# Cross attention: the projected queries of a slot are copied whole to SBUF before they are split

## The reference

```python
# x (8, 1024, 512), ctx (8, 64, 512), 16 heads of 32
Q = (x @ w_q.T).reshape(B, S, 16, 32).transpose(0, 2, 1, 3)
K = (ctx @ w_k.T).reshape(B, -1, 16, 32).transpose(0, 2, 1, 3)
V = (ctx @ w_v.T).reshape(B, -1, 16, 32).transpose(0, 2, 1, 3)
scores = jnp.einsum('bhqd,bhkd->bhqk', Q, K) / np.sqrt(32)
attn = jax.nn.softmax(scores, axis=-1)
c = jnp.einsum('bhqk,bhkd->bhqd', attn, V).transpose(0, 2, 1, 3).reshape(B, S, 512)
y = c @ w_o.T + b_o + x
mu, var = mean(y), mean((y - mu) ** 2)        # over the last axis
out = (y - mu) * rsqrt(var + 1e-5) * gamma + beta
```

## Time and profile before

| | us |
|---|---|
| median of 3 runs | 547.06 (547.06 to 550.45) |
| the profiled execution | 547.24 |
| its span | 545.3 |
| PE busy | 530.1 |
| DVE / POOL / ACT busy | 434.7 / 421.7 / 381.7 |

### The profile page before, as it was taken

One profiled execution on the slowest core, in us unless ns is written; L12 is line 12 of the kernel. 1 busy time (PEld: TensorE's weight loads), 2 busy tenths in 40 slices (PEclk: granted clock), 3 DMA queues, 4 the chain that ended last, 5 costly groups with the idle time before them and its releaser, 6 DMA issues.

```text
span 545.3 us, 12514 instructions
## 1 busy us (share of the span) xinstructions
PE 530.1 (97%) x4522; PEld 401.3 (74%) x4522; DVE 434.7 (80%) x877; ACT 381.7 (70%) x739; POOL 421.7 (77%) x387
## 2 busy tenths in 40 slices
PE   8999999999999999999999999999999999999994
PEld 6765587778777777777787778777877877787663
DVE  7876768778877877787778778877877787778897
ACT  7647767767676777677677767676777677666683
POOL 1726868888888888888888888888888888877755
PEclk9999999999999999999999999999999999999998
DMA  8943224333333332333244323333333332222112
GB/s 310 273 146 92 82 83 129 91 105 120 109 90 126 120 101 93 127 125 102 85 128 129 103 84 124 114 109 99 121 108 95 120 121 64 66 78 82 46 68 110
DMA packets 56750, 61.11 MB, mean 112 GB/s; under 512 B 29169, under 2 KB 29169, under 8 KB 56689
## 3 DMA queue, kind: packets, MB, share of 16 engines
q1 hardware_dynamic: 56688, 60.32, 35.3%
HBM read 39.58 MB, written 16.78 MB: 103 GB/s over the span
## 4 chain that ended last, share of the span: by engine, by line
PE 93%; DVE 2%; issue 2%; ACT 1%; DMA 1%; SPq 0%; DVEq 0%; ACTq 0%
PE ps_q L420 32%; PE ps_o L426 28%; PE ps_s L379 12%; PE ps_s L352 8%; PE ps_q L286 5%; PE ps_s L363 3%; PE ps_o L286 3%; PE ps_s L286 2%; PE ps_s L293 1%; DMA max_rows<-max_turned 1%; DVE stats L775 1%; DVE z L771 1%; DVE y L797 0%; DVE q_lo L686 0%; ACT q_hi L509 0%
## 5 line engine op out<-in xcount | busy, mean ns | idle before, releaser
L420 PE MATMUL ps_q<-x_hi,wq_lo 64*128 64x512 f32 x448 | 179.3, 400 | 4.8 <-DVE q_lo L686 0.4
L426 PE MATMUL ps_o<-wo_hi,c_lo 64*128 64x512 f32 x448 | 181.0, 404 | 0.0
L426 PE MATMUL ps_o<-wo_hi,c_hi 64*128 64x512 f32 x448 | 175.3, 391 | 0.0
L420 PE MATMUL ps_q<-x_lo,wq_hi 64*128 64x512 f32 x448 | 175.2, 391 | 0.0
L420 PE MATMUL ps_q<-x_hi,wq_hi 64*128 64x512 f32 x448 | 175.1, 391 | 0.0
L426 PE MATMUL ps_o<-wo_lo,c_hi 64*128 64x512 f32 x448 | 174.7, 390 | 0.0
L420 PEld LDWEIGHTS ps_q<-x_hi,wq_lo 64*128 64x128 f32 x448 | 82.7, 185 | 57.1 <-DVE z L771 51.7
L928 POOL TENSOR_TENSOR y<-y,gamma_row 128x512 f32<-128x512 f32 x60 | 78.3, 1306 | 58.7 <-ACT y L574 58.7
L906 POOL TENSOR_TENSOR c_lo<-c_raw,c_hi 128x512 fp32r<-128x512 f32 x63 | 81.3, 1291 | 27.5 <-ACT c_hi L509 27.5
L771 DVE TENSOR_TENSOR z<-ps_o,x_raw 128x512 f32<-128x512 f32 x59 | 40.8, 692 | 73.7 <-PE ps_o L426 73.3
L900 POOL TENSOR_TENSOR x_lo<-xT_raw,x_hi 128x512 fp32r<-128x512 f32 x60 | 77.8, 1297 | 12.5 <-ACT x_hi L509 12.5
(11 more groups left out here) (106 smaller groups left out, 1088.8 us busy)
## 6 DMA issues: line engine op xcount, KB each, us to landing
xT_raw<-in_xT SPq DMA_DIRECT2D x64, 256.0 KB, 2.9
x_raw<-in_x SPq DMA_DIRECT2D x64, 256.0 KB, 2.8
out<-y SPq DMA_DIRECT2D x64, 256.0 KB, 2.0
max_rows<-max_turned SPq DMA_DIRECT2D x128, 16.0 KB
ctx_raw<-in_ctxT SPq DMA_DIRECT2D x4, 256.0 KB, 4.6
wk_raw<-in_wkT SPq DMA_DIRECT2D x4, 256.0 KB, 4.8
wq_raw<-in_wqT SPq DMA_DIRECT2D x4, 256.0 KB, 5.8
wv_raw<-in_wvT SPq DMA_DIRECT2D x4, 256.0 KB, 6.8
```

Of the source, the lines that this page charges most:

```text
L420: return nc.tensor.matmul(ps_q[:, 0, :], w[l][half, k, dims], x_[r][half, qc % 2, k, :], start=(half is lower and k == 0 and step == 0), s ...
L426: return nc.tensor.matmul(ps_o[:, 0, :], cx[l][half, k, tile], wo[r][half, k, :], start=(half is upper and k == 0 and step == 0), stop=(ha ...
```

## The change

From slot 8 on (`COPIED`), ACT first copies the projected queries whole from the bank `ps_q` to `q_raw` in SBUF (`copy_queries`, one more ACT instruction per slot, 56 in all). PE waits for that copy (`q_copied`) instead of for `q_lo` before it begins the next projection. `q_hi` and `q_lo` are both made from `q_raw`. The lists of all engines are also rearranged. On ACT `normalise` moves behind the inversion of the sums, the exponentials ahead of `negate_max`, and the copy stands ahead of the inverse deviation. On DVE `q_lo` moves from the end of a slot to behind the transpose of the scores, and `divide` directly behind it; the statistics move behind `turn_max`. On POOL `c_lo` moves ahead of `add_bias`. At the end `store(62)` stands ahead of `store(63)`.

```diff
--- before.py
+++ after.py
@@ -24,6 +24,7 @@
     OUT_LAG = 7
     SPLIT_AHEAD = 5
     BY_VECTOR = (57, 58, 61, 63)
+    COPIED = OUT_LAG + 1
     WARM = 10
     SCALE = float(DK) ** -0.5
     EPS = 1e-5
@@ -73,6 +74,7 @@
         xT_raw = sb("xT_raw", [P, KT, CHUNK], fp32)
         x_hi, x_lo = sb("x_hi", [P, 2, KT, CHUNK], fp32r), sb("x_lo", [P, 2, KT, CHUNK], fp32r)
         q_hi, q_lo = sb("q_hi", [P, 2, CHUNK], fp32r), sb("q_lo", [P, 2, CHUNK], fp32r)
+        q_raw = sb("q_raw", [P, CHUNK], fp32)
 
         turned = sb("turned", [P, 2 * CHUNK], fp32)
 
@@ -146,7 +148,8 @@
         ctx_lo_done, wk_lo_done, wq_lo_done, wv_lo_done, wo_lo_done = (
             sem(f"{n}_lo_done") for n in ("ctx", "wk", "wq", "wv", "wo"))
         x_hi_done, x_lo_done = sem("x_hi_done"), sem("x_lo_done")
-        q_product, q_hi_done, q_lo_done = sem("q_product"), sem("q_hi_done"), sem("q_lo_done")
+        q_product, q_copied, q_hi_done, q_lo_done = (
+            sem(n) for n in ("q_product", "q_copied", "q_hi_done", "q_lo_done"))
         scores_done, turned_done, half_max_done = sem("scores_done"), sem("turned_done"), sem("half_max_done")
         upper_max_done, row_max_done, max_hi_done = sem("upper_max_done"), sem("row_max_done"), sem("max_hi_done")
         max_lo_done, max_turned_done = sem("max_lo_done"), sem("max_turned_done")
@@ -272,7 +275,7 @@
                 next_keys(t)
             fill_max_rows(SLOTS - 1)
 
-            for i in (55, 56, 57, 58, 59, 60, 61, 63, 62):
+            for i in (55, 56, 57, 58, 59, 60, 61, 62, 63):
                 store(i)
             for s in range(4):
                 sp.wait_ge(y_stored[s], 16 * TILES // 4)
@@ -303,9 +306,16 @@
                     if k == KT - 1:
                         mm.then_inc(keys_product, 1)
 
+            def queries_left(n):
+
+                if n >= COPIED:
+                    pe.wait_ge(q_copied, n - COPIED + 1)
+                else:
+                    wait(pe, q_lo_done, n + 1)
+
             def project_queries(n):
                 c, g = divmod(n, G)
-                wait(pe, q_lo_done, n)
+                queries_left(n - 1)
                 if g == 0 and c > 0:
                     pe.wait_ge(x_lo_done, KT * (c + 1))
                 for k in range(KT):
@@ -387,7 +397,7 @@
 
                 if ks[0] == 0:
                     if i == TILES - OUT_LAG:
-                        pe.wait_ge(q_lo_done, SLOTS)
+                        queries_left(SLOTS - 1)
                     elif i >= TILES - 2:
                         pe.wait_ge(c_raw_done, 62)
                     elif i < TILES - OUT_LAG:
@@ -527,8 +537,17 @@
 
             def queries_to_hi(n):
                 wait(act, scores_done, n - 1)
+                if n >= COPIED:
+                    act.wait_ge(q_copied, n - COPIED + 1)
+                    to_hi(q_hi[:, n % 2, :], q_raw[:, :]).then_inc(q_hi_done, 1)
+                else:
+                    act.wait_ge(q_product, n + 1)
+                    to_hi(q_hi[:, n % 2, :], ps_q[:, 0, :]).then_inc(q_hi_done, 1)
+
+            def copy_queries(n):
                 act.wait_ge(q_product, n + 1)
-                to_hi(q_hi[:, n % 2, :], ps_q[:, 0, :]).then_inc(q_hi_done, 1)
+                act.wait_ge(q_lo_done, n)
+                nc.scalar.activation(q_raw[:, :], ps_q[:, 0, :], ACT.Copy).then_inc(q_copied, 1)
 
             def negate_max(n):
                 act.wait_ge(row_max_done, n + 1)
@@ -632,23 +651,24 @@
 
             for t in range(OUT_LAG, SLOTS - 1):
                 i = t - OUT_LAG - 1
+                log_sums(t - 3)
+                invert_sums(t - 3)
                 if i >= 1:
                     normalise(i - 1)
-                log_sums(t - 3)
-                invert_sums(t - 3)
                 if t + SPLIT_AHEAD < SLOTS:
                     split_x(t + SPLIT_AHEAD)
+                exponentiate(t - 2)
                 negate_max(t - 1)
-                exponentiate(t - 2)
                 context_to_hi(t - 3)
+                copy_queries(t + 1)
                 if i >= 0:
                     invert_deviation(i)
                 queries_to_hi(t + 1)
 
 
-            normalise(54)
             log_sums(60)
             invert_sums(60)
+            normalise(54)
             exponentiate(61)
             context_to_hi(60)
             invert_deviation(55)
@@ -697,7 +717,8 @@
 
             def queries_to_lo(n):
                 dve.wait_ge(q_hi_done, n + 1)
-                to_lo(q_lo[:, n % 2, :], ps_q[:, 0, :], q_hi[:, n % 2, :]).then_inc(q_lo_done, 1)
+                to_lo(q_lo[:, n % 2, :], q_raw[:, :] if n >= COPIED else ps_q[:, 0, :], q_hi[:, n % 2, :]
+                      ).then_inc(q_lo_done, 1)
 
             for t in (kbd_hi, kbd_lo):
                 for half in range(2):
@@ -819,25 +840,27 @@
                 i = t - OUT_LAG
                 if i >= 1:
                     turn_scores(t - 1)
-                    half_maxima(t - 1)
+                    queries_to_lo(t)
                 divide(t - 3)
                 if i >= 1:
+                    half_maxima(t - 1)
                     fold_halves(t - 1)
+                turn_max(t - 1)
+                if i >= 1:
                     statistics(i - 1)
-                turn_max(t - 1)
                 add_residual(i)
-                queries_to_lo(t + 1)
 
 
             turn_scores(61)
+            queries_to_lo(62)
+            divide(59)
             half_maxima(61)
-            divide(59)
             fold_halves(61)
             turn_max(61)
             statistics(54)
             add_residual(55)
+            statistics(55)
             queries_to_lo(63)
-            statistics(55)
             turn_scores(62)
             divide(60)
             half_maxima(62)
@@ -950,8 +973,8 @@
                     scale(i - 1)
                 if t + SPLIT_AHEAD < SLOTS:
                     split_x(t + SPLIT_AHEAD)
+                context_to_lo(t - 3)
                 add_bias(t - 1)
-                context_to_lo(t - 3)
                 if i >= 0:
                     shift_mean(i)
```

## The result

| | before | after |
|---|---|---|
| median (6 runs each) | 547.06 | 556.96 |
| profiled execution | 547.24 | 558.03 |
| its span | 545.3 | 556.1 |
| PE / POOL busy | 530.1 / 421.7 | 535.9 / 442.4 |

The ratio after to before is 1.0174, with a 95% interval of 1.0144 to 1.0204: slower by 1.7%, where 551 us and 0.8% were forecast.

What follows compares the result with a forecast made beforehand. PE, waiting for `q_lo`, was taken to bound the kernel; afterwards POOL's loop would: 50 × 8.00 − 1.6 − 393.5 = +4.9, less 0.8 for 5 other slots, on 547.24: 551 us, range 539 to 560 (8 in 10).

Steps and rivals of the forecast that it cites:

- What bound the kernel before, and what was removed: PE waits for `q_lo` behind each combination; the copy removes 0.15 us in 55 slots, −8.3 us, slot 7.72.
- The copy on ACT, cost 0: One more 0.60 us ACT instruction per slot fits into ACT's 0.75 us wait; the logarithm stays near 1.20.
- DVE, cost 0: `divide` ends near 3.8 instead of 4.05, so PE's scores don't wait; up to 0.1 per slot if late.
- the hold: DVE's `q_lo`, now with two SBUF operands, and POOL's instructions wait for each other's end: 0.40 us per slot on POOL.
- The price that decides: `q_lo` reading both operands from SBUF always meets a running POOL instruction, lengthening POOL's loop by 0.40 to about 8.00 us.
- POOL's loop without a hold: Closed loop from `shift_mean` through ACT's `normalise` and back: 7.59 us, 0.13 under PE's 7.72, so not binding.
- 1.2 or more as a sign: If the forecast is right, `q_lo` on DVE shows a mean near 1.2 us or more instead of 0.69.
- PE's slack, 1.6 us once: POOL's lateness reaches PE only through ACT, DVE and z, whose idle time absorbs 1.6 us, once.
- The step that failed: In the tail, later scaling and the swapped last stores each cost under 1 us, taken as 0.
- No hold at all (539): Rival: POOL is not delayed, all 55 slots run at 7.72, 539 us; chance 0.16.
- The full hold (565): Rival: `q_lo` keeps POOL out for all 0.69 us, loop 8.28, +18, 565 us; chance 0.15 for 556 and more.

Runs made afterwards that it cites:

- experiment 1: Changed kernel, but DVE's `q_lo` (slots 8 to 62) compares with one operand from PSUM, leaving out the true `q_lo`: 541.53 us, ratio 0.9889 to the kernel before.
- experiment 2: Changed kernel, but POOL adds the bias to only 32 of 512 columns: 539.79 us, ratio 0.9863 to the kernel before.
- experiment 4: Changed kernel, computing everything, with `scale`, ACT's `normalise` and SP's stores moved later, and POOL's tail reordered: 539.85 us, ratio 0.9856 to the kernel before.
- runs 5 and 6: Kernel before plus one unused DVE instruction per slot ahead of z: a subtraction with two SBUF operands (555.95 us), then a transpose with one (547.3 us).
- Experiment 3: Kernel before with one move alone, ACT's `normalise` behind the inversion of the sums, in loop and tail: 551.16 us, ratio 1.0079.
- experiment 7: Changed kernel with SP's stores behind the copies of the maxima and `c_lo(60)` and tile 55's shift ahead of `scale(55)`: 554.2 us, ratio 1.0125 to the kernel before.

## Why the prediction was right or wrong

**What bound the kernel before, and what was removed: right.** PE's 0.15 us per slot behind `q_lo` was real and went away wherever nothing else came in its place: 1.02 us behind the combination and slots of 7.72 in experiments 1, 2 and 4, and in the changed kernel's own first slots.

**The copy on ACT, cost 0: right.** It takes 0.60 us and ends 0.26 into the slot; the logarithm still starts at 1.20 in experiment 1. In the changed kernel it starts at 1.65, because ACT waits for the late statistics.

**DVE, cost 0: right in experiments 1 and 4, not quite in the changed kernel.** With z late by 0.8 us by the hold's loop, DVE's list is late too, and the division again holds PE's scores. It doesn't add to the slot, because POOL sets its length anyway; it only shows as another place where PE waits out the same time.

**The price that decides: the mechanism right, the size too small.** POOL's loop without a hold was put at 7.59, and the slots of 7.72 in experiment 1, in which POOL is idle for 1.06 us around `normalise` instead of the 0.93 of the closed loop, agree: 7.72 less the spare 0.13 is 7.59. The hold was put at 0.40 and is 0.45: I let the shorter `q_lo` (0.69 against 0.75) end 0.49 behind POOL's instruction, and it ends 0.54 behind it, as the longer ones did. 8.04 against 8.00 is 2 us over 50 slots. `q_lo` takes 1.02 us, where I had named 1.2 or more as a sign. The page "SBUF — State Buffer" of the Trainium skill, section "Who interferes with whom", names the right pair of instructions, and runs 5 and 6 bear it out. By the words "fully blocks" of that page of the Trainium skill it would be 0.69 (an estimate, with the length of `q_lo`); the changed kernel's trace shows 0.45 to 0.48 added to POOL's addition of the bias (1.29 alone), and no slot of any run more than 0.52.

**PE's slack, 1.6 us once: right.** `normalise` drifted from 2.97 to 4.65 into the slot over the first six slots, by 0.31 to 0.36 in each, before PE felt it. That is 1.68 us. (The part of z in it was 0.64 by the rows, 0.38 against 1.02, and not 0.5; the sum came out all the same.)

**The step that failed: "In the tail, scaling comes later and the last stores are swapped; both are smaller than 1 us, and I take 0."** The tail costs 2.6 us (less 0.6 behind it, which goes with the order of the last stores: 19.9 to 20.0 us pass from the last combination to the end in the five runs that have the new order, 20.5 to 20.6 in the five that have the old one). I had not followed `normalise`'s 2.8 us through POOL's list to `c_lo(60)`, from there by the single `c_raw` to `divide(61)`, and down DVE's list to the statistics of tile 56. Experiment 3 shows this by the one move, experiment 7 that it can be mended. Nor had I walked SP's queue: the store of y waits for `scale` and stands ahead of the copies of the maxima, which are issued 0.94 us later by it. That leaves no room for the odd copy that takes 4.5 us, and one fell on a slot where PE sets the pace: 9.05 us where I had 7.72. Why a copy is sometimes late stays open; that it fell there is chance, and only its price follows from the lists.

Together: +4.1 forecast; 0.04 × 50 = 2.0 for the hold, 9.05 − 7.72 = 1.3 for the late copies of the maxima, 2.6 − 0.6 = 2.0 for the tail, make 9.4 of the measured 9.6.

**The rivals.** No hold at all (539) isn't what the change does: experiment 1 had to take the hold away for slots of 7.72, and experiment 4 had to open the loop. The full hold (565) would make POOL's loop 8.28, and it is 8.04. The measured 556.96 lies inside the range of 539 to 560, but where I had given 0.15, and I had tied that chance to the full hold. It got there by other terms: 3.3 us of the tail and the late copies, which no rival of mine had. So the range held in part by luck.

## What to carry to other kernels

Copying a PSUM tile to SBUF to free its bank gives a later DVE instruction on it a second operand in SBUF, and here POOL then waited for that instruction: where POOL is near its limit in a closed loop, count the wait. Here it was about 0.45 us of POOL's time for each instruction of 0.69 us. Look for a closed loop between two engines before trusting a busy share: POOL, at 77% of the span before and 80% after, had 0.28 us to spare in a slot before and none after, and moving the work that waits (`scale`) behind work that doesn't made room for the same hold at no cost. When an instruction is moved to a later place, follow it to the end of the program and through the DMA queue too; steady state tells only of the loop.

## What the runs showed of the hardware

The hold is nearly symmetric, and in these runs its price doesn't depend on which instruction of POOL it is. A held instruction on DVE (0.69 to 0.75 us alone) ends 0.54 to 0.56 us behind the end of POOL's. The next one on POOL ends 1.16 behind the end of DVE's where it takes 1.29 alone, in the product with gamma, the addition of the bias and `c_lo` alike, and `shift` ends 0.13 behind it where it takes 0.26 alone (experiments 2 and 4). So each ends as if it had begun 0.13 to 0.20 us before the other's end. An instruction that isn't held itself can still hold the next: in experiment 2 `q_lo` keeps its 0.65 us, and POOL's `shift` grows to 0.72.

In most slots at POOL's pace the copies of the maxima (two of 16 KB) had landed by 3.2 us after their issue in the changed kernel; in two slots of its loop PE waited for them until 4.16 and 4.5 us, and in one of experiment 7 until 4.47, with no store issued in the 5.35 us ahead of them. What makes these late, no run here shows.
